# Two product banks in the projection; masked copies and table products moved within a head's step of the attention

## What is computed

```
h = einsum('bhid,oi,od->bho', x, weighted_sum, weight)
q, k, v = split(norm(h) @ Wq + bq), ..k.., ..v..          # 16 heads of 16
scores  = q @ k.T / scale
c2p     = take(q @ pos_k.T, rel + SPAN) / scale            # by distance
p2c     = take(k @ pos_q.T, -rel + SPAN).T / scale
ctx     = softmax(scores + c2p + p2c) @ v
h       = h + ctx @ Wo + bo
h       = h + experts(norm(h))
```

## Time and profile before

| | |
|---|---|
| time, median of 3 runs | 4985.87 us (4980.09 to 4990.47) |
| time of the profiled execution | 5008.23 us |
| its span | 5006.5 us |
| busy in the span: TensorE matmul, VectorE, ScalarE, GpSimd | 4532.3, 3435.2, 2670.4, 1784.1 us |
| projection / attention / rest, in the span | to about 965 / to about 4180 / to 5006 us |
| DMA, mean over the span | 308 GB/s |
| granted TensorE clock, mean | 0.955 |

### The profile page before, as it was taken

One profiled execution on the slowest core, in us unless ns is written; L12 is line 12 of the kernel. 1 busy time (PEld: TensorE's weight loads), 2 busy tenths in 40 slices (PEclk: granted clock), 3 DMA queues, 4 the chain that ended last, 5 costly groups with the idle time before them and its releaser, 6 DMA issues. The chain is left out here.

```text
span 5006.5 us, 106625 instructions
## 1 busy us (share of the span) xinstructions
PE 4532.3 (91%) x29894; PEld 3224.8 (64%) x30324; DVE 3435.2 (69%) x9091; ACT 2670.4 (53%) x5075; POOL 1784.1 (36%) x4431
## 2 busy tenths in 40 slices
PE   6999999599999999999999999999999997883699
PEld 5777777366666666666666666666666665673566
DVE  3333333388888878878888878887888886776511
ACT  1222222277666666666666666766776774441111
POOL 1222222244444444444444444444444442330032
PEclk9999999799999999999999999999999999885599
DMA  5888888899999999999999999999999996662033
GB/s 171 276 278 275 276 282 272 289 382 376 381 369 372 365 364 377 377 364 364 362 360 377 377 364 376 379 379 363 382 377 378 380 371 204 208 210 86 2 95 81
DMA packets 684182, 1541.83 MB, mean 308 GB/s; under 512 B 50212, under 2 KB 286164, under 8 KB 683476
## 3 DMA queue, kind: packets, MB, share of 16 engines
q1 hardware_dynamic: 674646, 1523.26, 84.2%
q0 software_dynamic: 6144, 8.52, 1.0%
q10 hardware_dynamic: 2816, 3.41, 0.3%
HBM read 753.82 MB, written 781.21 MB: 307 GB/s over the span
## 5 line engine op out<-in xcount | busy, mean ns | idle before, releaser
L1039 DVE CUSTOM_DVE_ANT_1 a_scored<-a_ps_m_s,a_bias 128x512 f32<-128x512 f32 x2048 | 1394.1, 681 | 532.0 <-PE a_ps_m_s L908 503.5
L977 ACT ACTIVATE a_probsT<-a_ps_m_t 128x512 f32<-128x512 f32 x2048 | 1226.2, 606 | 954.9 <-PE a_ps_m_t L917 954.6
L917 PE MATMUL a_ps_m_t<-a_ident,a_scored 128*128 128x128 f32 x8192 | 1261.2, 277 | 0.7 <-ACT a_probsT L977 0.5
L917 PEld LDWEIGHTS a_ps_m_t<-a_ident,a_scored 128*128 128x128 f32 x8192 | 938.0, 141 | 437.7 <-DVE a_scored L1046 350.4
L971 ACT ACTIVATE a_skew_in<-a_ps_m_tab 128x512 f32<-128x512 f32 x2048 | 1125.3, 614 | 99.9 <-DMA d_skew<-a_skew_in 62.0
L1046 DVE TENSOR_SCALAR a_scored<-a_scored,a_top_of 128x512 f32<-128x512 f32 x2048 | 1023.4, 519 | 0.5
L863 POOL TENSOR_SCALAR_AFFINE_SELECT a_bias<-a_bias 128x128 f32<-128x128 f32 (+2 forms) x2560 | 943.3, 397 | 71.9 <-POOL a_bias L863 63.1
L854 POOL COPY a_bias<-a_high 128x128 f32<-128x128 f32 (+1 forms) x1024 | 347.3, 369 | 1654.5 <-DMA a_bias<-d_skew 1654.0
L908 PE MATMUL a_ps_m_s<-a_ident,a_bias 128*128 128x128 f32 x5120 | 897.0, 273 | 41.7 <-DVE a_top_of L1039 9.0
L894 PE MATMUL a_ps_m_tab<-a_tabs,a_stack 128*128 128x256 bf16 x4096 | 710.7, 276 | 109.8 <-ACT a_skew_in L971 53.2
L908 PEld LDWEIGHTS a_ps_m_s<-a_ident,a_bias 128*128 128x128 f32 x5120 | 690.3, 141 | 174.5 <-issue 2.9
(11 more groups left out here) (192 smaller groups left out, 3595.5 us busy)
## 6 DMA issues: line engine op xcount, KB each, us to landing
d_skew<-a_skew_in SPq DMA_DIRECT2D x512, 1024.0 KB, 8.0
a_bias<-d_skew SPq DMA_DIRECT2D x512, 896.0 KB, 8.2
a_stack<-d_stack SPq DMA_DIRECT2D x256, 512.0 KB, 8.7
p_xt<-in_xT SPq DMA_DIRECT2D x31, 2048.0 KB, 10.8
d_stack<-p_extra SPq DMA_DIRECT2D x64, 512.0 KB, 3.2
d_ctx<-a_ctx_sb SPq DMA_DIRECT2D x128, 256.0 KB, 7.8
d_stack<-p_part_q SPq DMA_DIRECT2D x64, 384.0 KB, 2.8
d_stack<-p_part_k SPq DMA_DIRECT2D x64, 384.0 KB, 3.4
```

The costliest lines, as they stand in the source:

```text
L917: mm = pe.transpose(m_t[:, k % 2, t * P:(t + 1) * P], scored[:, hh % SCORED, t, k * P:(k + 1) * P], ident[:])
L977: nc.scalar.activation(turned_at(hh // GH, hh % GH, k), m_t[:, k % 2], ACT.Exp, scale=SCALE).then_inc(turned, 1)
L1039: nc.vector.tensor_tensor_reduce(split(scored[:, hh % SCORED, t]), split(m_s[:, t % 2]), extra, 1.0, -3.0e38, ALU.add, ALU.max, top_of[:, ...
```

## The change

Three edits.

- Projection: the second half of the value product goes to the second bank of `m_qk` instead of `m_v`. It no longer waits for `keep_v` of the first half. The second query product (m = 1), which is the next to write that bank, waits for both `keep_v` of the batch before.
- Attention, VectorE: `fill` of head n+1 stands behind the first sum of head n, ahead of the second, instead of behind the first subtraction.
- Attention, TensorE and ScalarE: the four table products of head n+5 and their copies stand in quarters 2 and 3 instead of 0 and 1. On ScalarE they follow the exponents of these quarters.

```
+    def v_bank(half):
+        return m_qk[:, 1].rearrange("p (t o) -> p t o", t=2) if half else m_v[:]
...
                 after(pe, qk_kept, CH * n + m - 1)
+                if m == 1:
+                    after(pe, v_kept, 2 * n)
...
-                    after(pe, v_kept, 2 * n + half)
+                    after(pe, v_kept, 2 * n + half - 1)
...
-                            mm = pe.matmul(m_v[:, t], xnT[:, c, at:at + P], wv[:, c], start=(c == 0),
+                            mm = pe.matmul(v_bank(half)[:, t], xnT[:, c, at:at + P], wv[:, c], start=(c == 0),
...
-                        if t < 2 and not (last and m >= NH):
-                            for part in (2 * t, 2 * t + 1):
+                        if t >= 2 and not (last and m >= NH):
+                            for part in (2 * t - 4, 2 * t - 3):
                                 tables(n + LEAD, b + m // NH, m % NH, part)
...
-                        if t < 2 and not (last and m >= NH):
-                            for part in (2 * t, 2 * t + 1):
+                        if t >= 2 and not (last and m >= NH):
+                            for part in (2 * t - 4, 2 * t - 3):
                                 keep_tables(n + LEAD, m, part)
...
                         add_bias(n, hh, t)
                         if t:
                             lower(n, hh, t - 1)
-                        if t == 1 and not (last and hh == NH - 1):
+                        elif not (last and hh == NH - 1):
                             fill(n + 1, (hh + 1) % NH)
```

More of the change, by code:

```diff
@@ L628, in keep_v @@
                     v_sb[:, 2 * half:2 * half + 2, :, 0:HD],
-                    m_v[:].rearrange("p t (h d) -> p t h d", d=HD),
+                    v_bank(half).rearrange("p t (h d) -> p t h d", d=HD),
                     bv_row[:].rearrange("p (h d) -> p h d", d=HD).unsqueeze(1).to_broadcast([P, 2, NH, HD]),
```

## The result

The changed kernel takes 4936.4 us (median of 5 runs, 4929.2 to 4939.0) against 4980.1 us before (5 runs on the same chip, 4965.7 to 4990.5). The ratio is 0.9907, with a 95% interval of 0.9888 to 0.9926: 46 us faster (37 to 56). The profiled execution of the changed kernel has a span of 4934.0 us and stands at its median. That of the kernel before stood some 28 us above its own, so the spans of the two profiles lie 72 us apart, and differences between them overstate the change by up to that.

A forecast was written before the change was run, and what follows sets the result against it. It took the engines' loop (6.15 us a head) as the bound, with the transfers' limit within 2%. Projection -6, attention -15 and loop edges -5 gave -26 us from the 4985.9 us median: about 4961 us, range 4900 to 5042.

The forecast's parts named there:

- the likeliest case alone: Whole kernel: transfers bound the attention and the gain is small, 4961 us, spread 4935 to 4985, chance 40%.
- The cap that the bytes were to put on it: Attention transfers: 2.33 MB a head at 377 GB/s allow 6.18 us a head, though the engines could run at 6.05.
- The engines' loop: Attention, TensorE, VectorE and ScalarE: time the engines need per head falls from 6.15 to about 6.05 us.
- The wait that takes the old one's place: Attention, VectorE: masked copies wait for GpSimd's selections in the slow stretch, as spare time falls from 4.6 to 0.8 us.
- the third rival: Attention: the table path (write, read, selections, masked copies) becomes the bound; slower, 5031 to 5052 us, chance 30%.
- The projection: Value product in two banks: the wait moves to the next batch's turn, 0.2 us a batch, about 6 us gained.
- the -15 us of the attention: Attention: heads off the loop edges go from 6.21 to 6.18 us, the pace at 377 GB/s, over 512 heads.
- the engine-bound case: Attention: the engines set the pace, gaining 0.10 to 0.18 us a head, about 4910 us; sign 380 GB/s or more; chance 15%.
- The loop edges: Attention: behind each of five edges the engines run ahead at 6.05 us a head, about 1 us an edge, -5 us.

The follow-up runs named there:

- with fewer bytes: Each table read 128 KB shorter, in three kernels: kernel before 4953.1 us, changed kernel 4902.4 us, kernel with only the masked copies moved 4849.7 us.
- the copies alone: The kernel before with only the masked copies (fill) moved behind the first sum: 5001.3 us, ratio 1.0044.
- held writes: SP holds each table write until the next head's first score product is done: kernel before 4961.3 us, kernel with only the masked copies moved 4930.9 us.
- one score product too long: Kernel with bank, early masked copies and held table write, held until the next head's second score product instead of first: 5167.6 us.

## Why the prediction was right, point by point

The forecast was 4961 us, 25 us or 0.5% faster than the median it started from; 4936 lies inside the range, and faster had the largest chance, 0.48. The gain was forecast at little over half its size. It lies at the fast end of the likeliest case alone (4935 to 4985). The direction was reasoned, from an engines' loop that gets shorter. The cap that the bytes were to put on it was not where it was put, and that the number lies inside owes something to the width of the range.

**The engines' loop.** The steps held to a few hundredths. Second and third score product were put at 2.00 and 2.98 us into the head and are at 1.96 and 2.94. The table write was put at 7.35 and leaves at 1.34 into the next head, which at 6.03 us a head is 7.37. The loop was put at 5.97 and, with the context copy, 6.05; with fewer bytes a head takes 6.03. That the fourth table part would wait for ScalarE at the head's end is in the trace with 0.37 us.

**The wait that takes the old one's place.** The room of the table path was put at 0.8 us, from 4.6, with the masked copies waiting for selections. They wait 337 us, 348 times; before they waited for selections once, 2.5 us. That this would make the kernel slower (the third rival) was wrong: the time fell, and what the last 128 KB cost is 34 us, 5 more than before.

**The projection.** 0.2 us a batch was forecast from the row of the normalisation's end, and a move of the wait to the turn, not its end. The trace shows exactly that move. The size was 11 us (bounds of the interval 2 and 20) against 6: the turn starts 0.18 us sooner behind the normalisation's end, as worked out, and its eight weight loads also take 0.86 us instead of 1.02 in the earlier trace rows, which the sum had not.

**The transfers.** The term that was mis-sized is the -15 us of the attention, that is, the pace that the DMA engines were to allow. I took 377 GB/s, 6.18 us a head, as the middle of three stretches, all from one execution that was 28 us slower than the kernel's median. Measured, the attention's part of the gain is about 35 us (46 less the bank's 11), where -15 and -5 were put. Two things were wrong behind the term. First, the old attention itself moves 380 and 383 GB/s in the two stretches that had 369 and 377, in the trace of the kernel with the bank alone, and takes 6.14 us a head there. The cap was set under what the old order already reached. Second, the three rates are not samples of one capacity. The 377 was read where a head takes 6.14 us, which is the engines' own loop (6.12 to 6.15 with fewer bytes): there the engines asked for no more. The 391 was read in the last round, where their loop is 6.03 us.

So two limits lie close together, as the prediction had it, but in most heads of the kernel before the nearer one was the engines' loop. It fell by 0.09 to 0.12 us in a head of the looped rounds, and the transfers took hardly more than before. The stage moves 377 GB/s; 372 to 376 was forecast, and 380 or more was to be the sign of the engine-bound case. The outcome stands between the two cases.

**Why the transfers don't take the gain back.** This is only in part shown. With the copies alone they do: 152 us for the last 128 KB. The third rival had noted that the queue is slower when engines wait on it, and concluded that the tighter table path would lead there. The changed kernel's path is tighter and costs 34 us. A write two microseconds later and copies two microseconds earlier leave 19.8 us for write, read and selections, so write and read can't grow to the 18.5 us of the earlier trace rows unless the masked copies wait. In the changed kernel the landings sum to 15.8 at the median, against 17.7 with the copies alone.

That the moment at which a write is issued counts is shown by the added waits: held writes make two kernels faster, by 70 and by 14 us, with no work removed. That it counts through the depth of the queue is argued and not shown. For it: 390 GB/s at 8.1 us to landing and 364 at 9.9 in one execution. Against it: 386 GB/s at 9.1 us in the same execution, and 384 GB/s over a whole stage with the landing times of the kernel before. How transfers of different kinds follow each other changes along with the depth, and no run separates the two.

**The loop edges.** -5 us was put down for running ahead behind an edge. The edge stretch is 32 loads in 56 us before and after. The term stood for the heads behind the edges, and no run separates it from the rest of the attention's gain.

The DMA page of the Trainium skill (DMA: Bandwidth & Descriptors, Bandwidth) puts 425 GB/s on very large loads with the neighbouring core idle. No stretch shown here passed 391. By that figure the transfers would have been no limit, and yet the last 128 KB a head cost 29 to 152 us. The same section's limit of about 358 for a core's share of HBM is below the 364 to 391 of every stretch shown with all bytes and a share of 1.00.

## What to carry to other kernels

A DMA share of 1.00 doesn't say that the transfers alone set the pace: the kernel before has it, and 5.6% fewer bytes made it 0.6% faster. Take some bytes away, leave the work alone, and see what the time does. That gives the engines' own loop of each order and the price of the transfers, and the order that is best for the engines need not be best with all the bytes.

Before a slow stretch of one trace is made into a limit, look at a second execution of the same code. Here both stretches on which the cap rested ran faster in it. And before a rate is made into a limit, ask whether the engines asked for more.

When the transfers do cost time, try the moment of issue as well as the bytes: a later issue, or even an added wait, made two kernels faster here. Hold back only as long as the share stays at 1.00: one score product too long cost 253 us against the right length.

## What was not expected

- The same DMA engines, busy all the time on the same mix of transfers, moved 390 GB/s at 8.1 us to landing and 364 GB/s at 9.9 us within 350 us of one execution, and 386 GB/s at 9.1 us earlier in it.
- Removing 1.06 us from VectorE's part of the engines' loop in 512 heads, alone, made the kernel 22 us slower; a wait added to the same kernel made it 70 us faster.
